# A recommendation tower on one core: weight products ahead of everything, triple products in 154-column matmuls, the second layer by units of 32 rows, dense layers by chunk

## The reference

```python
x1[o,d] = sum_{m,h} W0[o,(m,h)] * X[m,d] * X[h,d] + b0[o]      # 128 outputs
x2[o,d] = sum_{m,h} W1[o,(m,h)] * X[m,d] * x1[h,d] + b1[o]     # 128 outputs
z = concat(x1.sum(d), x2.sum(d), dense_ctx)                    # 272 values
y = relu(relu(z @ W_top1 + b1) @ W_top2 + b2) @ W_top3         # 512, 256, 1
```

## Time and profile before

| what | us |
|---|---|
| median of three runs (lowest, highest) | 259.14 (256.49, 263.22) |
| the profiled execution: its own time | 258.26 |
| its span, first to last instruction | 256.5 |
| TensorE matmuls busy | 209.3 (82%) |
| GpSimd busy | 148.8 (58%) |
| VectorE busy | 127.2 (50%) |
| ScalarE busy | 84.4 (33%) |

### The profile page before, as it was taken

The page is one execution under the profiler, slowest core; times in us unless marked ns, Lnnn a source line. Parts: engine busy times, 40 slices in busy tenths (PEclk is TensorE's granted clock), DMA queues, the critical chain, the costliest instruction groups (busy, mean ns, idle before and its releaser), DMA issues.

```text
span 256.5 us, 10809 instructions
## 1 busy us (share of the span) xinstructions
PE 209.3 (82%) x5049; PEld 173.8 (68%) x5049; DVE 127.2 (50%) x194; ACT 84.4 (33%) x159; POOL 148.8 (58%) x142
## 2 busy tenths in 40 slices
PE   7897899499007889799898796979698896999995
PEld 6664667287006769688787584968697796899541
DVE  0559487666920866838649548173918641000000
ACT  2575447264202961413433313142313310100141
POOL 4778788877899778778778778777750000000000
PEclk9999799979856999999999999799889997999999
DMA  6811111112810111111111111111110000000000
GB/s 206 299 26 20 31 28 23 24 33 35 279 22 3 23 26 25 30 23 31 30 24 30 27 24 31 20 32 28 29 26 3 5 3 5 0 3 0 0 0 0
DMA packets 6564, 9.66 MB, mean 38 GB/s; under 512 B 2804, under 2 KB 3256, under 8 KB 6520
## 3 DMA queue, kind: packets, MB, share of 16 engines
q0 software_dynamic: 4096, 4.20, 9.1%
q1 hardware_dynamic: 2136, 4.19, 4.7%
q10 hardware_dynamic: 288, 0.59, 0.7%
HBM read 8.97 MB, written 0.00 MB: 35 GB/s over the span
## 4 chain that ended last, share of the span: by engine, by line
POOL 43%; PE 36%; issue 15%; DMA 3%; ACT 2%; DVE 0%; DVEq 0%; ACTq 0%; POOLq 0%
POOL rows L413 39%; PE psum L371 19%; PE psum L212 7%; PE psum L491 3%; PE psum L482 3%; DMA rows<-table,idx 2%; POOL t_sb L306 2%; POOL prod L261 2%; PE psum L280 1%; PE psum L193 1%; PE psum L286 1%; ACT t_sb L229 1%; DMA t_sb<-ids 1%; PE psum L474 0%; ACT prod L250 0%
## 5 line engine op out<-in xcount | busy, mean ns | idle before, releaser
L413 POOL DMA_INDIRECT rows<-table,idx x128 | 138.8, 1085 | 40.6 <-issue 38.1
L212 PE MATMUL psum<-prod,xx 64*32 64x77 f32 x4096 | 63.7, 243 | 23.7 <-POOL prod L261 13.4
L261 DVE TENSOR_TENSOR prod<-xx 128x1024 f32<-128x1024 f32 x62 | 73.7, 1220 | 6.8 <-ACT xx L241 4.0
L212 PEld LDWEIGHTS psum<-prod,xx 64*32 64x32 f32 x4096 | 51.4, 109 | 35.9 <-issue 16.2
L371 PE MATMUL psum<-t_sb,coef 128*128 128x128 f32 x552 | 67.9, 285 | 2.1 <-issue 2.1
L371 PEld LDWEIGHTS psum<-t_sb,coef 128*128 128x128 f32 x552 | 66.7, 202 | 2.4 <-issue 2.2
L229 ACT ACTIVATE t_sb<-psum 128x616 f32<-128x616 f32 x34 | 23.3, 685 | 79.8 <-PE psum L212 79.8
L226 DVE COPY t_sb<-psum 128x616 f32<-128x616 f32 x30 | 23.9, 798 | 49.8 <-PE psum L212 49.6
L292 ACT ACTIVATE t_sb<-psum 128x276 f32<-128x276 f32 x32 | 20.7, 647 | 18.2 <-PE psum L280 18.0
L241 ACT ACTIVATE xx<-psum 128x512 f32<-128x512 f32 x32 | 17.5, 595 | 24.2 <-PE psum L193 24.2
L280 PE MATMUL psum<-w0p_sb,w_sb 128*128 128x276 f32 x64 | 21.8, 423 | 1.2 <-DVE w0p_sb L592 0.6
(11 more groups left out here) (33 smaller groups left out, 99.9 us busy)
## 6 DMA issues: line engine op xcount, KB each, us to landing
rows<-table,idx POOLq DMA_INDIRECT x128
w_sb<-w1t SPq DMA_DIRECT2D x3, 512.0 KB, 7.0
w_sb<-top SPq DMA_DIRECT2D x2, 512.0 KB, 5.3
t_sb<-w0x ACTq DMA_DIRECT2D x1, 512.0 KB, 4.8
w0x_sb<-w0g SPq DMA_DIRECT2D x1, 512.0 KB, 3.8
w_sb<-w1t SPq DMA_DIRECT2D x1, 384.0 KB, 5.6
t_sb<-w0p SPq DMA_DIRECT2D x1, 276.0 KB, 5.0
w_sb<-w1t SPq DMA_DIRECT2D x1, 128.0 KB, 4.8
```

The source lines that it names most:

```text
L212: last = pe.matmul(bank(TG + 2 * (v % 2) + r, n * COLS, COLS, 32 * (2 * e + k), M), xx[s % 2][D * r:D * (r + 1), x:x + M], prod[2 * (s % 2 ...
L261: last = dve.tensor_tensor(at(p, e * COLS, [[2 * COLS, SUB], [HALF, SHIFTS], [1, HALF]]), at(x, x0, [[M, SUB], [0, SHIFTS], [1, HALF]]), a ...
L413: pool.indirect_dma_start(rows[:, c:c + D], None, table[:, :], bass.IndirectOffsetOnAxis(ap=idx[:, g:g + 1], axis=0))\
```

## The change

What it does, part by part:

- **Weight products first.** All 32 pair products, then all 32 cross products, over seven PSUM banks. The transposes of unit 0 stand after pair 23, those of unit 1 after cross 15. ScalarE makes most of the copies, VectorE twelve. The load of `w0x` moves from ScalarE's DMA queue to the end of the `w1t` loads on SyncE's.
- **Fold in halves, on VectorE alone.** The half k = 0 after 48 products, the half k = 1 after all; the coefficient transposes of the first four groups wait for the first piece of the second half only. GpSimd keeps only its gathers.
- **Triple products of 154 columns.** The two neighbouring 77-column operands that shared a stationary operand become one of 154: 16 matmuls per group where 32 were. The result lies otherwise in PSUM, so each group is taken out by four copies of 64 x 308 in place of one of 128 x 616; VectorE takes two of the four in odd groups (not in unit 0), ScalarE the rest.
- **Second layer by units.** `t_sb` of a unit (32 samples) is stationary and the coefficients (128 columns) move. The 77 terms go round four 128 x 32 tiles of the array, which leaves four partial sums on four quarters of the partitions. VectorE copies them out (`copy_acc`), two matmuls with four stacked identities add them (`sum_z`), ScalarE adds the bias (`copy_z`).
- **Order.** Unit 0's triple products, then the coefficients, then from unit 1 on: groups 0 and 1, half of `unit_cin` of the unit before, groups 2 and 3, the other half. Transposes are two units ahead up to unit 7 and one ahead from unit 8 on (`LATE`).
- **Dense layers by chunk.** Those of chunks 0 and 1 stand within the loop, at units 6, 7, 10 and 11 (`top_step`), those of chunks 2 and 3 behind it.

```diff
+LATE = 8
...
+        UNIT_ACC = (SPARE, TOP + 1)
+        W_BANKS = (TG, TG + 1, TG + 2, TG + 3, TOP, TOP + 1, SPARE)
...
+        PAIR_BY = [int(x % 3 == 1 and x < 24) for x in range(M)]
+        CROSS_BY = [int(x % 3 == 1 and 3 < x < 15) for x in range(M)]
...
+        COPIER = [0] * 8 + [(n + 1) % 2 for n in range(V_GROUPS - 8)]
...
+        def copier(group, p):
+            return int(p == 1 and group % 2 == 1 and group >= 4)
...
+        def wide_group(pe, u, v):
+            g = v // 2
+            p, x0 = prod[2 * (u % 2) + g], g * SUB // 2 * 2 * M + HALF
+            for n in range(2):
+                for i in range(2):
+                    j = 4 * (v % 2) + 2 * i + n
+                    x, y = x0 + j * 2 * M, 4 * j * COLS
+                    for k in range(2):
+                        for r in range(2):
+                            last = pe.matmul(bank(TG + 2 * (v % 2) + r, 2 * n * COLS, 2 * COLS, 32 * (2 * i + k), M),
+                                             xx[u % 2][D * r:D * (r + 1), x:x + M],
+                                             p[D * r:D * (r + 1), y + 2 * k * COLS:y + 2 * (k + 1) * COLS],
+                                             start=True, stop=True)
...
+            for p in range(2):
+                if copier(4 * u + v, p) != n:
+                    continue
+                for e in range(2):
+                    src = at(psum, (TG + 2 * (v % 2)) * BANK + e * COLS, [[1, COLS], [BANK, 2], [2 * COLS, 2]], D * p, D)
+                    dst = at(t_sb, t_at(u) + v * GROUP + 4 * p, [[CHUNK, COLS], [2, 2], [1, 2]], D * e, D)
+                    last = copy(dst, src)
...
+        def unit_tile(pe, u, j, n, col, w, start, stop):
+            c = t_at(u) + col * CHUNK
+            return pe.matmul(bank(UNIT_ACC[u % 2], n * O, O, UNIT * j, UNIT), t_sb[:, c:c + UNIT], w,
+                             start=start, stop=stop, tile_position=(0, UNIT * j))
...
-                    if g == FOLD_AT:
-
-                        products(pool, 0, 3, 1, 0)
-                        products(pool, 0, 3, 1, 1).then_inc(pool_prod, 1)
-                        pool.wait_ge(u_pairs, M)
-                        pool.wait_ge(u_cross, M)
-                        fold_first(pool, POOL_SHIFTS, pool_step)
-                        pool.wait_ge(pool_step, 1)
-                        fold_second(pool, POOL_SHIFTS, pool_step)
...
+            for x in range(M):
+                pair_product(pe, x)
+                if x == 23:
+                    transpose_rows(pe, 0)
+            for x in range(M):
+                cross_product(pe, x)
+                if x == 15:
+                    transpose_rows(pe, 1)
...
+            for v in range(4):
+                t_group(pe, 0, v)
+            transpose_rows(pe, 2)
             for n in range(V_GROUPS):
...
+            for u in range(1, ALL):
+                for g in range(2):
+                    t_group(pe, u, 2 * g)
+                    t_group(pe, u, 2 * g + 1)
+                    if g == 1 and LATE <= u + 1 < ALL:
+                        transpose_rows(pe, u + 1)
+                    unit_cin(pe, u - 1, 2 * g)
+                    unit_cin(pe, u - 1, 2 * g + 1)
+                    if g == 0 and top_step(u, 2) is not None:
+                        l1(pe, top_step(u, 2))
+                    if g == 0 and top_step(u, 3) is not None:
+                        l3(pe, top_step(u, 3))
+                if u >= 2:
+                    sum_z(pe, u - 2)
+                if u + 2 < LATE:
+                    transpose_rows(pe, u + 2)
+                if top_step(u, 2) is not None:
+                    l2(pe, top_step(u, 2))
...
             for part in range(4):
-                cin(pe, c, c % 2 * COLS * CHUNK, part)
...
+                unit_cin(pe, ALL - 1, part)
+                if part == 1:
+                    sum_z(pe, ALL - 2)
+            l1(pe, END - 1)
+            sum_z(pe, ALL - 1)
+            l2(pe, END - 1)
+            l1(pe, END)
+            l3(pe, END - 1)
+            l2(pe, END)
+            l3(pe, END)
...
+            for u in range(1, ALL):
                 for g in range(2):
+                    act_copy_t(act, u, 2 * g)
+                    act_copy_t(act, u, 2 * g + 1)
...
+                if LATE <= u + 1 < ALL:
+                    for g in range(2):
+                        act_xx(act, u + 1, g)
+                        act_gram(act, u + 1, g)
```

More of the change, by code:

```diff
@@ new lines, in wide_group, with t_group, copy_t @@
+            return last
+        def t_group(pe, u, v):
+            if v % 2 == 0:
+                pe.wait_ge(gram_ready, 2 * u + v // 2 + 1)
+                pe.wait_ge(prod_ready, 2 * u + v // 2 + 1)
+            for n in range(2):
+                wait(pe, t_copied[n], copied(n, 4 * u + v - 1))
+            last = wide_group(pe, u, v)
+            last.then_inc(t_done, 1)
+        def copy_t(eng, copy, n, u, v):
+            if u == UNITS and v < 2:
+                eng.wait_ge(coef_tr, V_GROUPS)
+            if u >= 2 * UNITS:
+                eng.wait_ge(unit_done, u - 2 * UNITS + 1)
+            eng.wait_ge(t_done, 4 * u + v + 1)
+            for p in range(2):
[5 more added lines that the diff above has]
+                    last = copy(dst, src)
+                last.then_inc(t_copied[n], 1)
@@ L286, in weight_products @@
[L286 to L297 removed]
+            w_bank_free(pe, M + x)
@@ new lines, in sum_z, with copy_z @@
+        def sum_z(pe, u):
+            if u == 0:
+                pe.wait_ge(stack_ready, 1)
+            pe.wait_ge(acc_copied, u + 1)
+            for n in range(2):
+                last = pe.matmul(bank(UNIT_ACC[u % 2], 2 * O + n * UNIT, UNIT), acc_sb[u % 2][:, n * O:(n + 1) * O],
+                                 stack[:, 0:UNIT], start=True, stop=True)
+            last.then_inc(z_done, 1)
+        def copy_z(act, u):
+            act.wait_ge(z_done, u + 1)
+            for n in range(2):
+                last = act.activation(at(w1_sb, z_at + n * B + u * UNIT, [[1, UNIT]]),
+                                      bank(UNIT_ACC[u % 2], 2 * O + n * UNIT, UNIT),
+                                      ACT.Identity, bias=cin_bias[:, 2 + n:3 + n])
+            last.then_inc(z_copied, 1)
@@ L395, in _ @@
             pool.wait_ge(idx_ready, 1)
-            for u in range(CHUNKS * UNITS):
+            for u in range(ALL):
                 s = u % UNITS
@@ new lines, in _ @@
+            products(dve, 0, 0)
+            products(dve, 0, 1)
+            for x in range(M):
+                if CROSS_BY[x] == 1:
+                    copy_cross(dve, dve.tensor_copy, x)
+            for n in range(2):
+                dve.wait_ge(u_copied[n], W_BY[:M + HALF].count(n))
+            fold_first(dve, 0)
+            dve.wait_ge(fold_step, 1)
+            fold_second(dve, 0, range(2 * SHIFTS))
+            products(dve, 1, 0)
+            for n in range(2):
+                dve.wait_ge(u_copied[n], W_BY.count(n))
@@ new lines, in _ @@
+            fold_first(dve, 1)
+            dve.wait_ge(fold_step, FOLDED)
+            for i in range(SHIFTS):
+                fold_second(dve, 1, (i, SHIFTS + i))
+            copies = [n for n in range(V_GROUPS) if COPIER[n] == 1]
+            for n in copies[:2]:
+                copy_coef(dve, dve.tensor_copy, n)
+            products(dve, 1, 1)
+            for n in copies[2:]:
+                copy_coef(dve, dve.tensor_copy, n)
+            dve.wait_ge(ident_ready, 1)
+            dve.tensor_tensor(at(stack, UNIT, [[UNIT, 2], [1, UNIT]]), at(ident, 0, [[UNIT, 2], [1, UNIT]]),
+                              at(ident, 2 * UNIT, [[UNIT, 2], [1, UNIT]]), ALU.add).then_inc(stack_step, 1)
@@ L653, in _ @@
+            dve.wait_ge(stack_step, 1)
+            dve.tensor_tensor(stack[:, 0:UNIT], stack[:, UNIT:2 * UNIT], stack[:, 2 * UNIT:3 * UNIT], ALU.add)\
+                .then_inc(stack_ready, 1)
             dve.wait_ge(small_in_sb, 32)
             dve.tensor_scalar(cin_bias[:, 2:4], cin_bias[:, 0:2], float(D), None, ALU.mult).then_inc(bias_ready, 1)
-            for c in range(1, CHUNKS):
-                chunk(lambda q, s, ahead: step(q, s, ahead, q % 2 * COLS * CHUNK), c, final=c == CHUNKS - 1)
@@ L658, in _ @@
-            dve.wait_ge(l3_done, 1)
-            for j in range(2, 4):
-                last = dve.tensor_copy(at(prod[3], 0, [[1, B // 4]], 32 * j, 1), bank(L3, 0, B // 4, 32 * j, 1))
-            last.then_inc(l3_ready, 1)
+            for u in range(1, ALL):
+                for g in range(2):
+                    dve_copy_t(dve, u, 2 * g + 1)
+                    if u + 1 < LATE:
+                        products(dve, u + 1, g)
+                    if u >= 2 and g == 0:
+                        copy_acc(dve, u - 2)
+                for g in range(2):
+                    if LATE <= u + 1 < ALL:
+                        products(dve, u + 1, g)
@@ L664, in _pairs @@
+            copy_acc(dve, ALL - 2)
+            copy_acc(dve, ALL - 1)
 def _pairs():
```

557 lines of the change are left out of this document (232 added, 325 removed).

## The result

The changed kernel takes **247.03 us** (245.59 to 248.69, 6 runs) where the kernel before takes 260.54 us in the same series (254.74 to 265.12, 6 runs). The ratio is **0.963**, with a 95% interval of 0.957 to 0.970: 3.7% faster. Some executions of a kernel are slower, at a lower granted clock, and the ratio leaves those out, so it is not the quotient of the two medians. I had forecast 223 us, with a range of 210 to 237. The direction was right, the size not: of the 36 us forecast 13.5 were gained by the medians, and about 9.5 by the ratio.

The account below looks back on a forecast made before the run. The gathers were taken to bound the first three quarters, TensorE the rest. Unit 15's transposes at about 192 us plus a 31.6 us tail gave a 223.6 us span, about 225 us, stated as 223, range 210 to 237.

Parts of the forecast that it names:

- The 9.3 us of GpSimd's folding: Gathers: GpSimd's 9.3 us of pair products and folding goes, so the gathers no longer run that much later.
- 4.5 us for `unit_cin`: Second layer: a unit's 154 records on four tiles side by side take 4.5 us.
- about 9.1 us a unit up to unit 7: Loop, units 1 to 7: TensorE's groups, second layer, transposes, `sum_z` and idle sum to 9.1 us a unit.
- changes of tile shape: Loop: four more TensorE drains a unit for tiling changes, estimated at 0.4 to 0.8 us a unit, outside the sum.
- unit 1 at 58: Start of the loop: weight products, fold and coefficients done at 58 us, when unit 1 starts; about 92 before.
- Case C: Rival in `unit_cin`, chance 0.06: 128 x 32 tiles don't run beside each other, 17.9 us a unit, 428 us, slower.
- Transposes of unit 15 ... about 192: Units 8 to 15: chain of 9.9 us a unit from 123 us gives 195.5, taken as about 192.
- the tail, 31.6 us: From unit 15's transposes to the end: 29.5 us of work plus about 2.1 of output, 31.6 us.
- the gathers at 177.5: GpSimd: last gather issued at 177.5 us, landed at about 180.5, with 4 us allowed either way.
- columns, not records: Triple products: if columns set the time, halving records gains nothing beyond stalls; 1.4 us taken for a pair of groups.
- Case A: Rival, chance 0.27: gathers stay the bound to the end, span 212, time 214 us.
- Case B: Rival, chance 0.07: ScalarE becomes the bound, 64-partition copies at 0.685 us, 10.3 us a unit, time about 250 us.

Follow-up runs that it names:

- e1: Changed kernel with LATE 16 in place of 8, so rows are transposed two units ahead throughout: 232.55 us, ratio 0.906 to the kernel before.
- e2: Changed kernel with the next unit's `xx` and first gram piece ahead of ScalarE's copies of groups 2 and 3: 232.49 us, ratio 0.902 to the kernel before.
- e4: Changed kernel with the first dense layer's dense part at 128 rows (112 of zeros) instead of 16: 242.93 us, ratio 0.934 to the kernel before.
- e7: LATE = 16 kernel with VectorE's fold left out but for one element per piece: 226.44 us, ratio 0.874 to the kernel before.
- e3: Changed kernel with 77-column triple products and one copy per group put back: 280.69 us, 8.9% slower than the kernel before.
- e6: As e3, but from unit 1 on only 38 of the 77 columns computed, instructions unchanged: 281.86 us.

## Why the prediction was wrong

**Right, in the same steps as put.** The 9.3 us of GpSimd's folding gone; 4.5 us for `unit_cin` (2.53 + 2.10 at the full clock); ScalarE's 64-partition copies at 0.42 (0.421); the pair of groups at 1.4 (mostly 1.3 to 1.6); about 9.1 us a unit up to unit 7 (8.5 to 8.9 in units 2 to 4), so that unit 8's transposes came at 123 (123.23). I can't tell from this whether the changes of tile shape, which I had priced at 0.4 to 0.8 us a unit and left out of the sum, cost anything, since the sum held 0.9 us of idle.

**Right by luck: unit 1 at 58.** It started at 57.96, but by other steps. The weight products were over at 36.3 (forecast 39) and the fold at 43.5 (forecast 48). Then TensorE waited until 44.49 for unit 2's rows, whose last gather the fold had held up for 6.7 us, and from the first coefficient transpose at 45.40 on it took 12.6 us, where I had 11 (47 to 58).

**Case C did not come.** 128 x 32 tiles do run beside each other, 154 records in 4.6 us where one at a time would take 17.9, and their weight loads are hidden. The rule of the Trainium skill that I weighed there ("TensorE: Matmul & The Clock Gate", Part 3, The mechanism), that loads overlap only with matmuls of another row group, does not hold for these tiles either: L386's loads and matmuls, all of 128 rows, follow each other every 30 ns. The same section of the Trainium skill also lets a load into a background weight buffer be pulled ahead of matmuls, which would fit these rows; no run shows such a buffer.

**Wrong: "Transposes of unit 15 ... about 192".** They came at 208.4. This is the step that failed. The mechanism, a chain through ScalarE, VectorE and TensorE, was there and was the bound, as e1 and e2 show; its size was off. I counted 9.9 us a step, seven times, 3.2 for dense layers, and took 3.5 off. The seven steps took 85.1 us in place of my 69:

- ScalarE's six copies stand in the chain for 2.3 us and not 1.6 (seven times 0.7). The prediction gives no working for its 1.6; six copies at its own 0.40 are 2.4.
- The first half of `unit_cin` is 84 of the 154 records and takes 2.5 us at the full clock, where I had 2.2 (seven times 0.3). With these two the step is 10.9, as in units 9 and 14.
- Within it TensorE waits for instructions in two of the steps, 0.96 and 0.77 us. I had no term for that.
- In two steps the granted clock falls, and they take 12.2 us in place of 10.9. I had no term for that either.
- The dense layers took about 4.6 and not 3.2.
- I took 3.5 us off the sum for idle that "not every unit has". But the chain's wait for VectorE was there in every step: 2.0 to 2.3 us in five of the seven, 1.8 in one, and less (0.62) only where a dense step filled it. The sum as worked out was the better one.

**Wrong: the tail, 31.6 us.** It was 36.7. The second half of the last `unit_cin` but one is over 14.3 us behind the transposes, where I had 12.2, most of it the third fall of the clock. From there to the end of unit 15's `unit_cin`, with the sums and a wait of 0.65 us for ScalarE, it is 6.6 us (forecast 4.8). The l1 behind it was counted at 2.8 us and took 4.1, for the changes of tiling that e4 takes away; I had weighed them for the groups and not for the 16-row matmuls.

**Wrong sums.** 223.6 + 1.8 + 0.9 is 226.3 and not 225, and I then took off 2 us more without a row for it. In case C the way from the forecast to 2% above the kernel before is 41 us, not 37.

**Wrong at a small price: the gathers at 177.5.** The last was issued 10 us later. I allowed 4 us for VectorE's load, and the fold alone took 7 (e7). In the changed kernel it cost the wait of 2.06 us ahead of the coefficients and nothing in the loop, where the rows waited for TensorE. It is the first thing that costs once the chain is gone.

**Wrong in the reasons: columns, not records.** I held the groups to be set by columns and gave the halved number of records no worth. e3 and e6 show that with 77 columns the loop is set by the instructions, at 14.4 to 15.0 ns each, 836 a unit. With 154 columns units 2 to 4 take 8.7 us each for 580 instructions, which is 15.0 ns as well, with TensorE busy for 25.8 of the 26.2 us; so whether columns or instructions set the changed kernel there is not shown. Had I been asked for the same change without the wide matmuls, I would have forecast a gain, as in e3's expectation, and it is a loss of 8.9%.

Case A (gathers the bound) did not come, but is what e1 turns the kernel into. Case B did not come.

## What to carry to other kernels

When a step is moved from "two ahead" to "one ahead", add up the whole path through all engines until it comes round again, with each engine's other work that stands in front of it in program order; here a loop in which TensorE was busy 9.9 us a unit (69.4 in seven) and each other engine under 8 ran at 12, and one constant or the order of three calls gave back 14.5 us. Part of what such a wait costs comes behind it, when the granted clock falls. Count the instructions of an engine as well as its columns: two parts of a change that alone lose (8.9%) or at least gain nothing may gain together, because one spends the instructions that the other saves.

## What the runs showed of the hardware

- TensorE's instructions, loads counted, did not come faster than one in 14.4 ns over tens of us (e3), though 128 of them (a pair of groups) come in 1.3 us; halving the columns of 3,840 of the records changed nothing (e6).
- They are loaded in packets of 16 KB, no two of which start less than 3.26 us apart in e3 and e6, and pauses of TensorE of up to 1.9 us (e3) end 1.2 to 1.5 us behind the landing of one, in 33 cases of 35.
- The granted clock fell to its lower level behind three of TensorE's seven waits of 1.8 to 2.3 us in the late loop and the tail of the changed kernel, and each fall cost 1.3 to 1.7 us.
- GpSimd's indirect DMA of 128 rows takes 0.94 us, but up to 6.7 us while VectorE runs tensor additions and products without a pause.
- Going to a 16-row matmul and back costs 0.4 us on top of the matmul's own time.
- Four 128 x 32 tiles, each with a 128-column fp32 matmul and a load of its own, give a record every 30 ns (154 in 4.6 us), four times the rate of full-width ones at 116 ns.
